# Summing the residual in PSUM by TensorE at the end of the first slot stage and of the softmax stage

## The reference

```
x = L0_attn_a_hidden_states                     # 16 x 1024 x 256, f32
x = x + attn_a(_layernorm(x))                   # convolutions, delta rule, router
x = x + ffn(_layernorm(x))                      # slot layer, first time
x = x + attn_b(_layernorm(x))                   # softmax attention, 16 heads of 16
x = x + ffn(_layernorm(x))                      # slot layer, second time

def _layernorm(x, axis=-1, eps=1e-05):
    m = jnp.mean(x, axis=axis, keepdims=True)
    v = jnp.var(x, axis=axis, keepdims=True)
    return (x - m) / jnp.sqrt(v + eps)

# end of the slot layer:
out = jnp.einsum('bts,bsd->btd', alpha, slot_values)     # 64 slots
return out @ wo.T + bo                                   # wo and bo are folded into the values
```

## Time and profile before

| | us |
|---|---|
| median of three timed runs | 8130.36 |
| lowest, highest | 8125.79, 8131.41 |
| the profiled execution, its own time | 8119.54 |
| span of its instructions | 8117.8 |
| busy in it: TensorE | 7320.9 (90%) |
| VectorE | 4790.0 (59%) |
| ScalarE | 3396.6 (42%) |
| GpSimd | 1778.1 (22%) |

### The profile page before, as it was taken

One profiled execution on the slowest core, in us unless ns is written; L12 is line 12 of the kernel. 1 busy time (PEld: TensorE's weight loads), 2 busy tenths in 40 slices (PEclk: granted clock), 3 DMA queues, 4 the chain that ended last, 5 costly groups with the idle time before them and its releaser, 6 DMA issues. The chain is left out here.

```text
span 8117.8 us, 122951 instructions
## 1 busy us (share of the span) xinstructions
PE 7320.9 (90%) x47966; PEld 4266.5 (53%) x47966; DVE 4790.0 (59%) x9348; ACT 3396.6 (42%) x6915; POOL 1778.1 (22%) x2690
## 2 busy tenths in 40 slices
PE   6899988999989999899999998998999989999999
PEld 3546455464554646546465464654645546465464
DVE  5565665656656566564665646656566654656546
ACT  3353543525335253352533525345253442534425
POOL 2212221122211222112221122212212212122221
PEclk9999999999999999999999999999999999999999
DMA  3011211212112021120211202121021210212102
GB/s 75 21 33 27 38 42 22 38 21 38 42 30 40 16 33 42 30 40 16 33 42 31 40 15 33 42 38 42 6 33 42 38 42 8 36 37 38 42 11 33
DMA packets 337771, 268.59 MB, mean 33 GB/s; under 512 B 213521, under 2 KB 276369, under 8 KB 337097
## 3 DMA queue, kind: packets, MB, share of 16 engines
q1 hardware_dynamic: 337148, 260.09, 17.0%
HBM read 48.71 MB, written 42.02 MB: 11 GB/s over the span
## 5 line engine op out<-in xcount | busy, mean ns | idle before, releaser
L1902 ACT ACTIVATE pre<-ps 128x512 f32<-128x512 f32 (+3 forms) x3072 | 1272.4, 491 | 724.3 <-PE ps L1890 718.8
L1827 DVE TENSOR_REDUCE sa_nm<-ps 128x2 f32<-128x1024 f32 (+4 forms) x1280 | 1389.1, 1115 | 277.7 <-PE ps L1808 138.1
L1890 PE MATMUL ps<-sa_qs,sa_ks 99*128 99x512 bf16 (+3 forms) x3072 | 792.1, 331 | 78.3 <-ACT pre L1902 58.4
L1909 POOL TENSOR_SCALAR_AFFINE_SELECT pre<-pre 128x512 f32<-128x512 f32 x512 | 325.0, 635 | 1699.4 <-ACT pre L1902 1696.7
L1808 PE MATMUL ps<-sa_ks,sa_qs 96*128 96x512 bf16 (+3 forms) x2560 | 626.1, 319 | 56.7 <-DVE sa_nm L1827 39.2
L1922 PE MATMUL ps<-pre,sa_va 128*17 128x512 f32 (+3 forms) x6144 | 645.6, 492 | 8.2 <-POOL pre L1909 8.2
L1890 PEld LDWEIGHTS ps<-sa_qs,sa_ks 99*128 99x128 bf16 x3072 | 257.1, 97 | 652.5 <-ACT pre L1902 473.8
L318 PE MATMUL ps<-identb 128*128 128x512 bf16 x2272 | 552.6, 390 | 10.5 <-ACT dr_z L1156 10.5
L704 PE MATMUL ps<-rep,stack 128*32 128x512 f32 x4608 | 524.0, 606 | 9.0 <-DMA rep<-paths 8.7
L950 POOL TENSOR_TENSOR A<-paths 128x256 f32<-128x256 f32 x384 | 268.0, 726 | 793.7 <-DVE paths L1122 793.7
L291 ACT ACTIVATE xn<-x,shift,rstd 128x256 f32<-128x256 f32 x384 | 207.9, 593 | 375.6 <-POOL shift L286 375.6
(11 more groups left out here) (365 smaller groups left out, 13983.2 us busy)
## 6 DMA issues: line engine op xcount, KB each, us to landing
sa_qs<-sa_parts SPq DMA_DIRECT2D x288, 128.0 KB, 4.6
sa_ks<-sa_parts SPq DMA_DIRECT2D x288, 128.0 KB, 5.9
x<-in_x SPq DMA_DIRECT2D x17, 1024.0 KB, 5.5
rep<-paths SPq DMA_DIRECT2D x128, 128.0 KB, 2.4
bounce<-paths SPq DMA_DIRECT2D x32, 512.0 KB, 2.9
out_y<-x SPq DMA_DIRECT2D x32, 512.0 KB, 3.0
rep<-paths SPq DMA_DIRECT2D x128, 127.9 KB, 3.1
rep<-paths SPq DMA_DIRECT2D x128, 127.8 KB, 3.2
```

The source lines that it names most:

```text
L1827: nc.vector.tensor_reduce(nm[:, g % 2, op.c, op.t, op.j:op.j + op.heads], cols, AX.X, ALU.max, negate=True).then_inc(s.slot_free, 1)
L1890: last = nc.tensor.matmul(bank[:, off:], ks[0:QROWS, g % NBUF, j, kt * P:(kt + 1) * P], qs[0:QROWS, g % NBUF, j, n * BANK + off:(n + 1) * ...
L1902: nc.scalar.activation(pt[:, gs % 2, j, off:BANK], ring_bank(ring_use(gs, j))[:, off:], ACT.Exp, scale=RATIO).then_inc(s.ring_out, 1)
L1909: nc.gpsimd.affine_select(block, block, [[0, GH], [1, P]], ALU.is_ge, 0.0, base=0, channel_multiplier=-1).then_inc(s.masked, 1)
```

## The change

Where the first slot stage and the end of the softmax stage summed the residual on VectorE, the sum is now made in the bank of PSUM, by a product of the identity matrix with x1 that TensorE adds to the bank (`residual_pe`).

- In the first slot stage the four residual products open the banks, and the output products (L1526 of before) add to them. Three of them stand where the 16 keep-warm products were, the third behind a wait for `n_in`; the fourth stands behind the transposes of mem. The banks of the pairs are now 2, 3, 0, 1 (`out_bank`), in both slot stages, and the one-column product goes to bank 7.
- In the softmax stage two residual products add pairs 3 and 4 to late_slot: one behind the last sums, one behind the transposes of these sums.
- `norm_statistics` and ScalarE's normalising read these banks of PSUM in place of x1.
- VectorE copies the sum from PSUM into x1 afterwards (`keep_tokens_dve`), a pair at a time, behind a wait for ScalarE's normalising of that pair. In the first slot stage two of these copies stand before each of the two copies to xnT; in the softmax stage two stand between these.
- The adds (L309 in the first slot stage, L1973 for pairs 3 and 4) are gone.

```diff
+def tokens_of(bank):
+    return bank.rearrange("p (t d) -> p t d", t=2)
+def residual_pe(nc, k, bank, u, start=False):
+    return nc.tensor.matmul(bank, k.ident[:], k.x1[:, 2 * u:2 * u + 2, :].rearrange("p t d -> p (t d)"), start=start,
+                            stop=not start, skip_group_check=True)
+def keep_tokens_dve(nc, k, s, dve, bank, u):
+    dve.wait_ge(s.xn_normed, 2 * u + 2)
+    nc.vector.tensor_copy(k.x1[:, 2 * u:2 * u + 2, :].rearrange("p t d -> p (t d)"), bank)
...
@@ slot_ffn, TensorE @@
-                    keep_warm(nc, k, ps[:, 7, :], 16)
+                    residual_pe(nc, k, out_bank(0), 0, True)
+                    residual_pe(nc, k, out_bank(1), 1, True)
+                    pe.wait_ge(s.n_in, 1)
+                    residual_pe(nc, k, out_bank(2), 2, True)
...
                 last.then_inc(s.memt_ps, 1)
+                if store is None:
+                    residual_pe(nc, k, out_bank(3), 3, True)
                 pe.wait_ge(s.memt, 1)
...
@@ slot_ffn, VectorE @@
-                    add_with_statistics(nc, k, s, dve, settle, lambda u: ps[:, u, :])
+                    for u in range(T // 2):
+                        dve.wait_ge(s.out, u + 1)
+                        norm_statistics(nc, k, s, settle, tokens_of(out_bank(u)), u)
                     for n in range(NB):
+                        for u in (2 * n, 2 * n + 1):
+                            keep_tokens_dve(nc, k, s, dve, out_bank(u), u)
                         turned_dve(nc, k, ps, s, dve, 4, n)
...
@@ softmax_attention, TensorE @@
                 sums_pe(pe, AG * NSTEPS - 1)
+                residual_pe(nc, k, late_slot[:, 0, :], 2)
                 turn_sums_pe(pe, AG * NB - 1)
+                residual_pe(nc, k, late_slot[:, 1, :], 3)
...
@@ softmax_attention, VectorE @@
                 for u in (2, 3):
-                    add_out_dve(dve, settle, late_slot, u)
-                    norm_statistics(nc, k, s, settle, k.x1, u)
-                for n in range(NB):
-                    turned_dve(nc, k, ps, s, dve, RING_BANK, n)
+                    dve.wait_ge(s.out, u + 1)
+                    norm_statistics(nc, k, s, settle, tokens_of(late_slot[:, u % 2, :]), u)
+                turned_dve(nc, k, ps, s, dve, RING_BANK, 0)
+                for u in (2, 3):
+                    keep_tokens_dve(nc, k, s, dve, late_slot[:, u % 2, :], u)
+                turned_dve(nc, k, ps, s, dve, RING_BANK, 1)
```

More of the change, by code:

```diff
@@ L269, in norm_statistics @@
     for t in (2 * u, 2 * u + 1):
-        last = nc.vector.bn_stats(k.stats[:, t, :], x[:, t, :])
+        last = nc.vector.bn_stats(k.stats[:, t, :], x[:, t % 2, :])
     settle(last)
@@ L1488, in _ @@
                 pe.wait_ge(s.alpha_sum, 1)
-                nc.tensor.matmul(ps[0:SLOTS, 3, 0:1], alpha_sum[:], k.xn[:, 0, D:D + 1], start=True,
+                nc.tensor.matmul(ps[0:SLOTS, 7, 0:1], alpha_sum[:], k.xn[:, 0, D:D + 1], start=True,
                                  stop=True).then_inc(s.weighed, 1)
@@ L1525, in _ @@
                     pe.wait_ge(s.alphat, t // (BANK // P) + 1)
-                    last = nc.tensor.matmul(ps[:, t // 2, (t % 2) * D:(t % 2 + 1) * D], alphaT[:, t * P:(t + 1) * P],
-                                            values[:], start=(t % 2 == 0), stop=True, skip_group_check=True)
+                    last = nc.tensor.matmul(out_bank(t // 2)[:, (t % 2) * D:(t % 2 + 1) * D], alphaT[:, t * P:(t + 1) * P],
+                                            values[:], start=(t % 2 == 0 and store is not None), stop=True,
+                                            skip_group_check=True)
                     if t % 2:
@@ L1564, in _ @@
                 if store is None:
-                    normalise_and_turn(nc, k, ps, s, act, 4)
+                    normalise_and_turn(nc, k, ps, s, act, 4, {u: out_bank(u) for u in range(T // 2)})
             @block.vector
@@ L1597, in _ @@
                 dve.wait_ge(s.weighed, 1)
-                settle(nc.vector.tensor_scalar(wsum[:], ps[0:SLOTS, 3, 0:1], 1e-8, None, ALU.add))
+                settle(nc.vector.tensor_scalar(wsum[:], ps[0:SLOTS, 7, 0:1], 1e-8, None, ALU.add))
                 settle(nc.vector.reciprocal(wsum[:], wsum[:]))
@@ L1630, in _ @@
                         xs = k.x1[:, 2 * u:2 * u + 2, :].rearrange("p t d -> p (t d)")
-                        nc.vector.tensor_tensor(xs, xs, ps[:, u, :], ALU.add).then_inc(s.x_out, 1)
+                        nc.vector.tensor_tensor(xs, xs, out_bank(u), ALU.add).then_inc(s.x_out, 1)
             @block.gpsimd
@@ L2088, in _ @@
                 nc.scalar.activation(oT[:, 1, BANK:L], ps[:, RING_BANK, :], ACT.Copy).then_inc(s.ot1, 1)
-                normalise_and_turn(nc, k, ps, s, act, RING_BANK)
+                late_slot = slot_of(pe_use[0] - 2)
+                normalise_and_turn(nc, k, ps, s, act, RING_BANK, {u: late_slot[:, u % 2, :] for u in (2, 3)})
             @block.vector
```

15 lines of the change are left out of this document (8 added, 7 removed).

## The result

| | before, us | after, us |
|---|---|---|
| median of the timed runs | 8130.89 | 8049.32 |
| lowest, highest | 8125.79, 8161.39 | 8032.48, 8055.89 |
| span of the profiled execution | 8117.8 | 8030.8 |
| mean granted clock in it | 0.956 | 0.965 |

The ratio is 0.9889, its 95% interval 0.9859 to 0.9918: about 82 us faster, where 48 were forecast. Here are the page's totals of the changed kernel, for the earlier trace rows. L1547 is now the line of the output products, L2027 that of the next stage's first products.

A forecast was written before the change was run, and what follows sets the result against it. It took TensorE, busy 90%, as the main engine, with A ended by its queue and S by the norm chain; 11.2 + 37.1 = 48.3 us off 8130.4 gave 8082, range 8054 to 8118.

The forecast's parts named there:

- The cadence at A: First slot stage's end: without its add a pair costs VectorE 1.22 us, not 1.94; first transposes start 1.4 us earlier.
- A: End of the first slot stage, said to end by TensorE's own queue; forecast gain 0.70 us a sequence, 11.2 in all.
- Only 0.70 us of the 1.4 comes out: At A: keep-warm products at half clock delay the second transposes, leaving 0.70 us a sequence of 1.4.
- rival 3: At A the clock also comes back earlier, by half of 6.8 us: 27 us gained, 8055; chance 0.08.
- Residual products: At A and S: 0.86 us each on TensorE, expected to be covered, as are the copies on VectorE.
- S: End of the softmax stage, said to end by the norm chain; forecast gain 37.1 us over sixteen sequences.
- PSUM reads: BN_STATS and normalising reading PSUM at both places: taken as 0, bounds -1 to +7 us in all.
- The clock stays at 2.4 GHz through S: Softmax stage's end: residual products in TensorE's gaps keep the clock up, so the 6.8 us at half clock there go.
- Rivals 1 and 5: 1: clock falls at S as before, 8109, chance 0.20; 5: it falls before the residual products, 8146, chance 0.06.
- Rival 1: Clock falls at S as before; 0.76 us less 0.12 gained there a sequence, 21 in all, 8109; chance 0.20.
- 2.46 us at S: Softmax stage's end: last transposes start 2.46 us sooner in eleven sequences, 2.00 in five; 37.1 us together.
- Rival 2: Half-clock stretches further on take back half of the whole gain: 24 us left, 8106; chance 0.10.

The follow-up runs named there:

- e3: The kernel before with two idle f32 products put into TensorE's two gaps at the end of the softmax stage; 8100.3 us, ratio 0.9969.
- e4: The changed kernel without the softmax stage's two residual products, so the chain is short and the gaps are empty; 8091.3 us, ratio 0.995.
- e9: The kernel before with two idle f32 products in the gaps at S and 18 instead of 10 keep-warm products further on; 8090.3 us, ratio 0.9949.
- e2: The changed kernel with the softmax stage as before, so only the first slot stage's part; 8122.8 us, ratio 0.9998.
- e5: The changed kernel with six keep-warm products added in two gaps at the opening of the softmax stage; 8056.0 us, ratio 0.9899.
- e11: The changed kernel with 6 instead of 12 keep-warm products at A and 18 instead of 8 behind the second slot stage's last output products; 8056.6 us, ratio 0.9902.
- e10: The kernel before with 18 instead of 8 keep-warm products behind the second slot stage's last output products; 8146.0 us, ratio 1.0022.

## Why the prediction was right or wrong, point by point

- **The cadence at A**: 1.22 us forecast for a pair, 1.23 measured; the first transposes 1.4 us earlier, and 1.49 came out. Right.
- **"Only 0.70 us of the 1.4 comes out"**: the second transposes were to start 12.4 us after L1526; they start at 12.27. The whole of A takes 14.1 to 14.4 us in 12 sequences, 0.7 to 0.8 less. In the other four it takes 11.45 to 13.13: the clock came back earlier there (rival 3, its 0.08 now seen in a quarter of the sequences), or didn't fall. 20.5 us in all, where 11.2 stood in the sum.
- **Residual products**: 0.86 us each forecast. The six records of three start 0.43 us apart, the first two 0.53, so 0.86 and a tenth before the first. Neither they nor the copies are waited for at A, and at S the transposes of L2076 start 2.82 us after the last sums, where it was 2.80; the copies started at 361.41 and 363.84, forecast 361.5 and 364.0.
- **PSUM reads**: BN_STATS takes 420 ns from PSUM, 412 from SBUF; normalising takes 566 from PSUM, 592 from SBUF. The rows of the two sources in the changed kernel:

```profile
L270 DVE BATCH_NORM_STATS2 stats<-x x192: 400/412/430, 317.1 to 7979.1; 128x6 f32<-128x256 f32 x192
L270 DVE BATCH_NORM_STATS2 stats<-ps x192: 411/420/433, 356.5 to 7990.7; 128x6 f32<-128x256 f32 x192
...
L310 ACT ACTIVATE xn<-x,shift,rstd x192: 587/592/605, 319.5 to 7989.3; 128x256 f32<-128x256 f32 x192
L310 ACT ACTIVATE xn<-ps,shift,rstd x192: 556/566/583, 358.9 to 7993.4; 128x256 f32<-128x256 f32 x192
```

  The value of zero was right. As an estimate, the fixed costs in the errata table of the Trainium skill (VectorE: DVE Perf Modes) make a read of VectorE's 65 ns dearer from PSUM (120 cycles against 58); the trace has 8. The prediction put these 65 ns on every dependent read, but the table's row for ScalarE has PSUM as the cheaper source, 172 cycles against 224, and there the trace agrees in sign, with 26 ns.
- **"The clock stays at 2.4 GHz through S"**: so it did, in all sixteen, and e3, e4 and e9 show that the products in the gaps do it. L1991 took 1.99 us. Rivals 1 and 5 fall. Rival 1 had priced the chain alone too low: 0.76 us a sequence at S before its charge of 0.12 for the second residual product, where e4, without these products, shows 1.13.
- **2.46 us at S**: the last transposes start 7.39 after the first, 7.65 forecast; 2.72 us a sequence in eleven and about 2.2 in five, 40.7 in place of 37.1.
- **The sum**: this is the step that failed. It held 48.3 us for A and S, which gave 61.2 (A 9.3 more than its 11.2, S 3.6 more than its 37.1), and *nothing* for all else, which in the profiled pair gave 26 net: 14.9 lost in the softmax stage, 40.8 gained in the others by half clock that went from stages which the change doesn't touch. Rival 2 had only a loss for these stages, and rival 3 placed its gain at A. I had priced S's half clock where it stood and not asked what follows from its going: before, the next sequence's projections mostly opened with 6.8 us of half clock, after with 3.4. The nominal agreement of the forecast with A and S less the softmax stage's loss (61.2 - 14.9 = 46.3) is chance.
- **"Part is given back"**: right as a mechanism for A, where e2 leaves 5 us of 22 in the mean span (8131.6 to 8126.4, which can't be told from nothing), wrong for the whole.
- **The range** took its low end from a single extra at A. The placement of half clock alone moves this kernel more than that. e3, one kernel, ran ten times between 8083.4 at a mean clock of 0.964 and 8141.7 at 0.956. That is some 7 us for each 0.001 of mean clock. The 26 us net of the other stages had no term in my sum.

What stays open: why the fall moves to the delta rule in e5 and doesn't in e9, and so how much of the gain outside a given edit will bring. That there is one, with the clock held at S, rests on nine kernels against five. "Other" is 5008 to 5027 in seven of the nine, 5045 in e5 and 5014 in e11 (less the cost of its added products); where the clock falls at S or just behind it, it is 5034 to 5051 in four and 5031 in e10 (less the same). The averages are 5020 and 5042. So holding the clock at S goes with some 20 us outside on average; the rest of the changed kernel's 40 is not accounted for by it.

## What to carry to other kernels

Where an engine's clock follows its activity, a short product put into a gap ahead of a chain may be worth more than the instruction that it replaces, and the price of a fall is to be looked for in the stages behind it too: compare the half-clock time stage by stage, in both directions, before a sum is closed. Products put in to keep the clock up are also a queue; count how many of them still stand between a finished result and the work that waits for it, and leave as few as bring the clock back just ahead of the next stage (here four to six instead of twelve, 27 to 34 us of the medians). The idle of "issue" behind the last instruction of the stage could not be filled here: e10 paid 1.86 us a sequence for trying.

## What the runs showed of the hardware that was not expected

- The same work, as far behind the same first product, ran at 2.4 GHz to 34.0 us at least in all sequences before, and at 1.2 GHz from some 31.6 us on in 11 of 16 after. The difference that the trace shows is when the clock had last risen, about 2.6 us ahead of that product in place of 3.2 to 4.0.
- Executions of one kernel differ widely: e3's ten by 58 us, before's 57 by 101 (8096.7 to 8197.5). In e3 the times follow the mean granted clock; before's longest is an exception, with a clock of 0.914 and yet only 66 us above the mean.
- The clock fell at S (534.5) with no idle of TensorE above 0.81 us in the 7 us ahead of it, and in the softmax stage (401.3) with none above 0.89 us.
- ScalarE normalised 128 x 256 values from PSUM in 566 ns and from SBUF in 592 (medians of 192 records each).
- Two idle f32 products in gaps, which no result needs, took 16.3 us off S's sixteen passes (e3), and 19.6 with eight keep-warm products behind them (e9). Shortening its chain gave 18.1 (e4).
